# Residual graph layer on one core: in the last rows, a chunk of the plain sum ahead of the turn, and another order of VectorE's work on the last three rows

## The reference

```python
type_sum = adj @ x                                   # the plain sum, the same for a and b
attn_a = sigmoid(concat([type_sum, x], 1) @ Wa.T + ba)
attn_b = sigmoid(concat([type_sum, x], 1) @ Wb.T + bb)
h = x @ W_sa
scores = (h @ a_sa[0, :512])[:, None] + (h @ a_sa[0, 512:])[None, :]
e = where(adj != 0, exp(-leaky_relu(scores, 0.01)), 0.0)
x_a = (e / (e.sum(1, keepdims=True) + 1e-5)) @ h
x_b = adj @ (x @ W_gcnb) + b_gcnb
y = x + sigmoid(attn_a * x_a + attn_b * x_b)
out = layernorm(y)                                   # over the 512 features, eps 1e-5
```

## Time and profile before

| | |
|---|---|
| median of 3 runs | 962.42 us (961.98 to 964.37) |
| profiled execution, its own time | 962.28 us |
| its span, first to last instruction | 960.4 us |
| PE busy | 943.9 us, 98% of the span |
| DVE busy | 672.0 us, 70% |
| ACT busy | 440.7 us, 46% |
| POOL busy | 114.3 us, 12% |

### The profile page before, as it was taken

The page is one execution under the profiler, slowest core; times in us unless marked ns, Lnnn a source line. Parts: engine busy times, 40 slices in busy tenths (PEclk is TensorE's granted clock), DMA queues, the critical chain, the costliest instruction groups (busy, mean ns, idle before and its releaser), DMA issues. The chain is left out here.

```text
span 960.4 us, 13001 instructions
## 1 busy us (share of the span) xinstructions
PE 943.9 (98%) x4368; PEld 783.6 (82%) x4368; DVE 672.0 (70%) x1264; ACT 440.7 (46%) x798; POOL 114.3 (12%) x328
## 2 busy tenths in 40 slices
PE   9999999999999999999999999999999999999996
PEld 6888887788788888888888888888888888888875
DVE  5979878875767676676676676685675675565667
ACT  5656644442544443543453453443543443454432
POOL 0000000220120120120120120120120120111112
PEclk9999999999999999999999999999999999999999
DMA  8677532333333433433434433333433333333320
GB/s 264 185 201 227 170 105 77 109 98 99 112 105 94 124 91 107 120 96 102 121 95 105 119 100 99 110 105 93 121 105 94 109 111 87 88 105 88 94 72 33
DMA packets 139555, 109.00 MB, mean 113 GB/s; under 512 B 10337, under 2 KB 113633, under 8 KB 139489
## 3 DMA queue, kind: packets, MB, share of 16 engines
q1 hardware_dynamic: 138624, 106.74, 39.2%
q10 hardware_dynamic: 864, 1.44, 0.7%
HBM read 101.32 MB, written 6.83 MB: 113 GB/s over the span
## 5 line engine op out<-in xcount | busy, mean ns | idle before, releaser
L595 PE MATMUL bank<-e_hi,x_hi 128*128 128x512 f32 (+1 forms) x728 | 273.3, 375 | 1.4 <-DVE e_lo L774 1.1
L597 PE MATMUL bank<-e_lo,x_hi 128*128 128x512 f32 (+1 forms) x728 | 272.4, 374 | 0.0
L596 PE MATMUL bank<-e_hi,x_lo 128*128 128x512 f32 (+1 forms) x728 | 272.2, 374 | 0.0
L399 ACT ACTIVATE e_hi<-u,c_col 128x512 fp32r<-128x512 f32 (+1 forms) x182 | 126.0, 692 | 258.0 <-DVE u L762 115.2
L620 PE MATMUL bank<-x_hi,adj_r 128*128 128x512 f32 x572 | 225.0, 393 | 0.0
L621 PE MATMUL bank<-x_lo,adj_r 128*128 128x512 f32 x572 | 223.0, 390 | 0.0
L774 DVE SCALAR_TENSOR_TENSOR e_lo<-u,c_col,e_hi 128x512 fp32r<-128x512 f32 (+1 forms) x182 | 130.0, 714 | 46.5 <-ACT e_hi L399 37.5
L595 PEld LDWEIGHTS bank<-e_hi,x_hi 128*128 128x128 f32 x728 | 137.0, 188 | 27.6 <-DVE e_lo L774 2.1
L406 ACT CAST adj_r<-raw 128x512 fp32r<-128x512 f32 (+1 forms) x180 | 105.1, 586 | 115.3 <-PE bank L621 98.8
L596 PEld LDWEIGHTS bank<-e_hi,x_lo 128*128 128x128 f32 x728 | 137.0, 188 | 24.9
L597 PEld LDWEIGHTS bank<-e_lo,x_hi 128*128 128x128 f32 x728 | 137.0, 188 | 24.6
(11 more groups left out here) (119 smaller groups left out, 848.3 us busy)
## 6 DMA issues: line engine op xcount, KB each, us to landing
raw<-adj_t_dram SPq DMA_DIRECT2D x158, 256.0 KB, 2.9
adj<-adj_t_dram SPq DMA_DIRECT2D x156, 256.0 KB, 2.9
out_dram<-y SPq DMA_DIRECT2D x24, 256.0 KB, 3.3
z1s<-x_dram SPq DMA_DIRECT2D x14, 256.0 KB, 5.2
adj<-adj_t_dram SPq DMA_DIRECT2D x26, 128.0 KB, 2.2
raw<-adj_t_dram SPq DMA_DIRECT2D x22, 128.0 KB, 2.4
z2s<-x_dram SPq DMA_DIRECT2D x6, 256.0 KB, 4.6
y<-x_dram SPq DMA_DIRECT2D x6, 256.0 KB, 3.8
```

The costliest lines, as they stand in the source:

```text
L399: nc.scalar.activation(e_hi[g % E_RING][:, 0:cols(b)], u[g % U_RING][:, 0:cols(b)], ACT.Copy, scale=c_col[:, j:j + 1]).then_inc(e_hi_ready, 1)
L595: nc.tensor.matmul(z1[k][:, 0:n], x_hi[:, j, kk], e_hi[s][:, 0:n], start=(j == 0), stop=False)
L596: nc.tensor.matmul(z1[k][:, 0:n], x_lo[:, j, kk], e_hi[s][:, 0:n], start=False, stop=False)
L597: ins = nc.tensor.matmul(z1[k][:, 0:n], x_hi[:, j, kk], e_lo[s][:, 0:n], start=False, stop=(j == TILES - 1))
```

## The change

Two reorderings of the tail; no instruction is added, dropped or given another size.

On PE, chunk 4 of row 25 comes before turn(24) and its wait. For that, ACT copies this chunk before it scales row 23; the copies of chunks 5 and 6 stay where they were.

On DVE, the low part of row 25's turned z2 (L1011, "the last z2") and `make_gates(25)` come directly behind `gate_dots(25)`. The three steps of `root(24)`, which stood ahead of them, follow behind the gates. `normalise(23)`, which stood there too, goes between the two halves of adding row 25's projected z2 (L1021). The two scalings `normalise_last(24)`, which stood behind `make_gates(25)`, go behind `spread(25)`, ahead of `root(25)`. The stores of rows 23 and 24 on SP wait for these scalings and keep their order.

```diff
@@ ACT
+            adjacency(chunk_number(LAST, LAST_FIRST))
             act.wait_ge(proj_done, 2 * (LAST - 2) + 1)
             scale_p1(LAST - 2, proj)
             z2_hi(LAST - 2)
             gate_exps(LAST - 1)
-            for c in range(LAST_FIRST, CHUNKS):
+            for c in range(LAST_FIRST + 1, CHUNKS):
                 adjacency(chunk_number(LAST, c))
@@ PE
+            sum_z2(chunk_number(LAST, LAST_FIRST))
             pe.wait_ge(zt_lo_ready, 2 * (LAST - 1))
             turn(LAST - 1, turned)
-            sum_z2(chunk_number(LAST, LAST_FIRST))
             project_z2(LAST - 2)
@@ DVE
             gate_dots(LAST)
-            root(LAST - 1)
-            normalise(LAST - 2)
             dve.wait_ge(zt_hi_ready, 2 * LAST)
             nc.vector.tensor_tensor(e_lo[2][:, :], z2[0][:, :], e_hi[2][:, :].bitcast(F32), ALU.subtract) \
                 .then_inc(zt_lo_ready, 1)
             make_gates(LAST)
-            normalise_last(LAST - 1)
+            root(LAST - 1)
             dve.wait_ge(p1_scaled, LAST + 1)
             nc.vector.scalar_tensor_tensor(last_y[LAST], bias_row[:, :], gates[:, LAST, 1:2], last_y[LAST], ALU.mult,
                                            ALU.add).then_inc(bias_added, 1)
             dve.wait_ge(bias_added, LAST + 1)
             for n, half in enumerate(HALVES):
+                if n == 1:
+                    normalise(LAST - 2)
                 dve.wait_ge(proj_done, LAST_Z1[LAST] + n + 1)
...
             spread(LAST, last_stats[:, :, :].rearrange("p n s -> p (n s)"), LAST + 2)
+            normalise_last(LAST - 1)
             root(LAST)
             normalise_last(LAST)
```

## The result

The changed kernel takes 959.07 us (median of 19 runs, 957.39 to 961.82), the kernel before 962.35 (median of 19, 960.40 to 965.50). The ratio is 0.9961 with a 95% interval of 0.9950 to 0.9972: 0.39% faster, 0.28% to 0.50%. Four executions of this study, of both kernels, took 981 to 3398 us and are left out of every ratio. The class doesn't fit: 0.68 was given to "within 0.3%" and 0.28 to "faster by more".

A forecast was written before the change was run, and what follows sets the result against it. PE bounds the first 925 us, DVE and PE in turn the tail. Gains of 0.91 + 0.13 + 0.15 + 1.60 less 0.12 make 2.67 us off 962.42, given as 959.8 us; range 958.8 to 961.0.

The forecast's parts named there:

- Part 1: Tail, chunk 4 ahead of turn(24): PE 1.93 us earlier, hidden in its wait; DVE 1.19 us earlier at the gate dots.
- 0.15 us more: Gate dots of row 25 on DVE: no longer waiting for ACT's z2s copy, they start 0.15 us closer to L897.
- that at L1002: DVE at L1002: its 0.16 us wait for PE goes, less 0.03 for a dependent start, 0.13 us won.
- Part 2: DVE's low part of the last z2 (L1011) directly behind the gate dots: starts 1.60 us earlier.
- What is moved: DVE tail: root(24) hidden while ACT scales row 25; normalise(23), 0.46 us, hidden in a 0.67 us idle, 0.2 to spare.
- The scaling beside POOL's power: Last wait of the tail: normalise_last(24) on DVE holds POOL's power, making L903 0.12 us later.
- three cases: L903 later by 0.04 us if nothing holds POOL's power, 0.12 if the first scaling does, 0.45 if both do.
- Rival 1: Last wait: POOL's power held by both scalings; gain 2.34 us, time 960.1; chance 0.15.
- rival 2: DVE doesn't follow PE's lead at L848 or the dots; gain only 1.5 us, time 960.9; chance 0.08.
- Rival 4: Slower: the early chunk copy waits for its load and holds ACT ahead of L453; up to 966 us; chance 0.04.
- rival 3: Over 0.3% faster, 959.4 or less: power not held (gain 2.75), 0.15 us more from L1016 or run scatter; chance 0.28.

The follow-up runs named there:

- part 1 alone: Kernel before with chunk 4 of row 25 and its ACT copy moved ahead of turn(24), DVE's order as before: ratio 0.9986 (0.9957 to 1.0016).

## Why the prediction was right or wrong

| behind L453, us | before | forecast won | after | won |
|---|---|---|---|---|
| product of row 23 on PE | 4.28 | 1.93 | 2.35 | 1.93 |
| L848, now L849 | 7.21 | 0.91 | 6.31 | 0.90 |
| L1002, now L1003 | 12.65 | 1.04 | 11.67 | 0.98 |
| gate dots of row 25 | 15.99 | 1.19 | 14.95 | 1.04 |
| L1011, now L1010 | 19.10 | 2.79 | 16.42 | 2.68 |
| second L1021, now L1022 | 23.01 | 2.79 | 20.34 | 2.67 |
| L903 of row 25, now L904 | 26.16 | 2.67 | 23.59 | 2.57 |
| end | 29.85 | 2.67 | 27.27 | 2.58 |

**Part 1** went as worked out: the chunk is hidden, PE gains 1.93 us, DVE follows by about 1. The term "0.15 us more" at the dots came to 0.06, and that at L1002 to 0.08 instead of 0.13: the gaps between DVE instructions were 0.11 and 0 where I had put 0.03 and 0.08 of overlap. **Part 2** went as worked out: 1.64 for 1.60. **What is moved** was hidden: root(24), and normalise(23) with the 0.2 us to spare; the run with row 24's scalings there too shows that this room was used up.

**The scaling beside POOL's power** cost 0.10 where I had taken +0.12, the middle of three cases; the runs with one column and with one long scaling show that this case is the right one. (The "0.85" given for the distance from L897 to L903 doesn't match the sum, which makes it 0.81 + 0.12 = 0.93; it measured 0.91.) Rival 1 (held by both scalings, 2.34) is excluded. So is rival 2 (part 1 swallowed): part 1 is worth 1.04 alone, and 2.58 - 1.12 = 1.46 once part 2 is in. Rival 4 didn't occur: the copy was ready 3.6 us before L453.

**The step that failed** is the one from the sum to the chances: "Forecast and rivals 1 and 2 are all within 0.3%: 0.68". The sum lay 0.22 us inside a border of 2.89, and I gave the whole of three cases to one side of it. That step put everything outside the terms of the sum at nothing, the scatter of two sets of runs included. What the runs showed in its place: the tail got 2.58 us shorter, inside the border and 0.09 from the sum, but the whole time 3.3 us, and 3.6 on average over four sets. The measured ratio so fell on the other side, as rival 3 had it, but not for its trace terms: the power was held, and L1016 (now L1015) came 2.68 us earlier like L1011. What remains is its "from the runs themselves". That the time lies in the range is in part luck, as the sum has no term for the last 0.7 us.

How much of the measured 0.39% is more than the tail's 2.58 us (0.27%, a ratio of 0.9973)? The four sets of the changed kernel give 0.9961, 0.9970, 0.9958 and 0.9969. Weighted by their intervals that is 0.9963, and 0.0007 to either side if the sets are independent, which they aren't quite. It is 1 us more than the tail. Ahead of L453 no profile settles it: L453 starts at 929.2 to 941.1 in the six profiles with the empty wait and at 929.6 to 937.3 in the thirteen with it filled, and ahead of L453 the change moves only the copy of chunk 4, into idle time of ACT, with the load behind it on SP, and the chunk's first matmul.

What the prediction didn't have among its rivals is that PE's idle time can cost more than its own length: the falls of the clock behind the 1.98 us, 1.7 us each, came in half of the profiles with this wait and in none with it filled. That would be the missing us, in direction and size. The granted clock of the executions moves the same way: in the three later sets it is 0.0003 to 0.0006 higher for the changed kernel than for the kernel before, 0.3 to 0.6 us of 960, but the standard errors are as large. And three things keep this cause from being shown. The kernel with the same place filled by useless work measured 1.0014 and 1.0000, which leaves room for 0.9991 but doesn't show it. The falls were seen on two chips only, and the one set of the changed kernel that ran on one of them has 0.9970, about what the tail gives. And the two profiles of the kernel before with whole times near 962 us, beside which the first set and the fourth (0.9961 and 0.9969) were measured, have no fall there. A comparison of two kernels with nearly the same tail shows how far sets can differ: 0.9982 with the x rows early, 0.9958 for the changed kernel on the same chip. So the tail's 2.58 us are shown, the falls behind the empty wait are shown in profiles of two chips, and whether they, scatter or something else make up the further 1 us stays open.

## What to carry to other kernels

Compare traces from an instruction that the change doesn't touch: here it gave a change of 0.27% to within 0.05 us from one profile, where 19 runs left 2 us open. Look at the granted clock of that stretch in every profile, though: behind a wait of PE there can be a fall that one profile happens not to have, and another chip may show it where the first didn't. When work is moved into a wait, look at who is being waited for: if it is POOL and the work is DVE's, the work can lengthen the wait, by the length of the single instruction more than by the sum. When a move wins nothing, follow what it delays to the engine that waits for it: here two additions on DVE held POOL, and through row 24's low part PE. And before giving a result to one side of a border of measurement, put its distance from the border beside the scatter of the sets, not beside the bounds of the sum.

## What the runs showed of the hardware

- POOL's power (128x1) took 0.55 us alone, 0.65 beside two DVE scalings of 256 columns, 0.80 beside one of 512; it ended 0.40 to 0.41 us behind the end of the scaling that it had met.
- DVE additions with both inputs in SBUF (L881, 1.27 us for two) lengthened POOL's moments of one row by 0.55 us. In the same place the changed kernel's POOL steps took 0.46 and 0.19 us, and 0.81 and 0.53 beside the additions.
- The granted clock fell to half in 3 of 6 profiles shortly behind a wait of PE of 1.9 to 2.0 us (until 941.71, 943.00 and 940.06), 1.7 us lost each time, and in none of 13 with that wait down to 0.2 us. All three were on two of the chips. Elsewhere in the 19 profiles it fell behind waits of 0.95 to 1.78 us (near 245, 391 and 675 us, 16 times), but never behind the wait of 1.5 us near 182 us. In the run with part 1 alone it fell behind another wait, of 2.05 us:

```profile
953.56 0.39 PE L645 MATMUL bank<-w_hi,e_hi 128*128 128x256 f32 x1 [2.05 <-DVE e_lo L1012]
```
